# Expert stage on TensorE: the row-column products of the next super between the output products of the preceding one

## What is computed

```python
t = _to_tokens(x)                                 # (32, 3136, 64)
t = t + ffn(_ln_t(t), gate_w, gate_b, w1, b1, w2, b2)

# ffn: every token x goes to the expert with the largest gate probability
idx = argmax(softmax(x @ gate_w + gate_b));  prb = its probability
hmid = relu(buf @ w1 + b1)                        # per expert: 64 -> 256
ybuf = hmid @ w2 + b2                             # per expert: 256 -> 64
y = ybuf[idx, pos] * prb * kept                   # kept: within the capacity
y = nan_to_num(y, nan=0, posinf=1e4, neginf=-1e4)
```

## Time and profile before

| what | value |
|---|---|
| median of 3 runs | 1895.83 us (1888.43 to 1896.14) |
| span of the profiled execution | 2079.0 us |
| expert stage in it, first to last hidden product | 1061.2 to 2036.4 us |
| TensorE busy, whole span | 1654.2 us (80%) |
| VectorE busy | 1482.2 us (71%) |
| ScalarE busy | 1206.3 us (58%) |
| GpSimd busy | 1048.5 us (50%) |
| mean granted TensorE clock, as a share of 2.4 GHz | 0.881 |

### The profile page before, as it was taken

One profiled execution on the slowest core, in us unless ns is written; L12 is line 12 of the kernel. 1 busy time (PEld: TensorE's weight loads), 2 busy tenths in 40 slices (PEclk: granted clock), 3 DMA queues, 4 the chain that ended last, 5 costly groups with the idle time before them and its releaser, 6 DMA issues.

```text
span 2079.0 us, 40865 instructions
## 1 busy us (share of the span) xinstructions
PE 1654.2 (80%) x10341; PEld 880.9 (42%) x10341; DVE 1482.2 (71%) x3641; ACT 1206.3 (58%) x4066; POOL 1048.5 (50%) x1052
## 2 busy tenths in 40 slices
PE   7998888888888878775058888888888888878884
PEld 1344433443333434443034444555555445445453
DVE  3488878878887878888135666787677777777675
ACT  3687877777777877765035554655455454455451
POOL 2116655655676656667524444554444444444442
PEclk7898989988899989886579999999999999999896
DMA  9136766554557554442164555777777677777786
GB/s 240 40 97 145 176 165 157 150 142 117 148 149 135 139 133 108 108 112 78 59 191 142 145 147 144 193 219 244 226 234 230 220 236 225 228 222 228 227 247 221
DMA packets 302207, 351.64 MB, mean 169 GB/s; under 512 B 48452, under 2 KB 252452, under 8 KB 295940
## 3 DMA queue, kind: packets, MB, share of 16 engines
q1 hardware_dynamic: 260644, 264.23, 47.2%
q0 software_dynamic: 41120, 85.81, 13.3%
q10 hardware_dynamic: 320, 0.33, 0.1%
HBM read 179.70 MB, written 180.01 MB: 173 GB/s over the span
## 4 chain that ended last, share of the span: by engine, by line
PE 37%; issue 16%; DVE 14%; another core or an unknown queue 11%; POOL 8%; ACT 6%; DMA 4%; SPq 2%; ACTq 1%; POOLq 0%; DVEq 0%
PE bank L821 9%; PE bank L831 8%; POOL pairs_by_group L490 6%; PE bank L812 3%; PE bank L730 3%; POOL X L484 3%; PE bank L692 2%; PE bank L839 2%; PE bank L789 2%; PE bank L740 2%; DMA X<-weights_by_group 2%; PE bank L763 2%; ACT X L975 2%; DVE Z L1250 1%
## 5 line engine op out<-in xcount | busy, mean ns | idle before, releaser
L521 POOL DMA_INDIRECT results_by_pair<-X,PAIRNO x462 | 461.2, 998 | 542.1 <-ACT X L980 420.6
L490 POOL DMA_INDIRECT pairs_by_group<-ROWS,idx x400 | 435.4, 1088 | 133.2 <-issue 113.9
L821 PE MATMUL bank<-X 64*128 64x256 f32 x1848 | 287.7, 432 | 60.6 <-issue 28.7
L975 ACT ACTIVATE X<-bank,X 128x256 f32<-128x256 f32 x693 | 284.6, 474 | 76.2 <-PE bank L821 58.9
L968 ACT ACTIVATE X<-bank 128x256 f32<-128x256 f32 x231 | 90.5, 392 | 389.9 <-remote 238.1
L484 POOL TENSOR_TENSOR X<-Z,X 128x448 f32 (+1 forms) x112 | 137.0, 1223 | 308.9 <-DVE Z L1266 290.9
L831 PE MATMUL bank<-X 128*64 128x256 f32 x1848 | 276.3, 424 | 6.9 <-ACT X L985 6.9
L812 PE MATMUL bank<-ident,X 128*64 128x128 f32 x1848 | 159.3, 294 | 145.5 <-DMA X<-weights_by_group 69.2
L821 PEld LDWEIGHTS bank<-X 64*128 64x128 f32 x1848 | 180.3, 200 | 114.7 <-issue 103.3
L730 PE MATMUL bank<-S,WB 128*128 128x448 bf16 x1008 | 227.9, 374 | 0.0
L1289 DVE TENSOR_SCALAR X<-bank,X 128x256 f32<-128x256 f32 x231 | 111.1, 481 | 131.8 <-PE bank L821 63.3
(11 more groups left out here) (209 smaller groups left out, 3006.5 us busy)
## 6 DMA issues: line engine op xcount, KB each, us to landing
X<-weights_by_group SPq DMA_DIRECT2D x231, 258.5 KB
X<-pairs_by_group SPq DMA_DIRECT2D x231, 134.0 KB
pairs_by_group<-PAD SPq DMA_DIRECT2D x15, 1742.0 KB
X<-in_x_dram SPq DMA_DIRECT2D x16, 1568.0 KB
block_output<-X SPq DMA_DIRECT2D x112, 224.0 KB, 1.9
ROWS<-block_output SPq DMA_DIRECT2D x16, 1568.0 KB
Z<-results_by_pair SPq DMA_DIRECT2D x16, 1568.0 KB
out_dram<-ROWS SPq DMA_DIRECT2D x16, 1568.0 KB
```

The lines of the kernel that those rows point to most:

```text
L490: pool.indirect_dma_start(rows, bass.IndirectOffsetOnAxis(ap=idx[0:m, p.odd, k:k + 1], axis=0), ROWS[0:m, p.odd, k, :], None).then_inc(s_s ...
L521: pool.indirect_dma_start(done, bass.IndirectOffsetOnAxis(ap=PAIRNO[:, u, j:j + 1], axis=0), RES[:, u, j, :], None,).then_inc(s_back[u], 16)
L821: mm(hidden(q), WR[b, ring, q // 2 * P:(q // 2 + 1) * P], XT[b, ring % 2, :], start=True, stop=True).then_inc(s_h, 1)
L975: last = A(HB[:, ring % 2, q, :], hidden(q), ACT.Relu, bias=WR[:, ring, at:at + 1])
```

## The change

Only TensorE's `super_pass` changes. The hidden products of super k come first in the pass. Behind them the four row-column products of super k+1 and the four output products of super k-1 stand alternately: row-column product 0, output product 0, row-column product 1, and so on. The waits that stood ahead of either group now stand together ahead of the joint one. The row-column product q and the output product q write the same half of the partitions. ScalarE, VectorE, GpSimd and SyncE keep their programs; lines behind the edit have numbers that are 7 higher (ScalarE's 968, 975, 980, 985 become 975, 982, 987, 992).

```diff
             def super_pass(k, ring, t=True, l1=True, l2=True, back=True):
-                if t:
-                    u = (ring + 1) % RING
-                    wait(pe, s_rt[u], (k + 1 - u) * (32 // RING) + 32)
-                    wait_apart(pe, s_xt, k + 1)
-                    for d in range(SUB):
-                        for h in range(2):
-                            last = mm(PT[h * C:h * C + C, d * P:(d + 1) * P], RTH[:, u, d, h, 0:C], ident[:, :],
-                                      start=True, stop=True)
-                    last.then_inc(s_pt, 1)
                 if l1:
                     wait(pe, s_xt, k + 1)
                     wait(pe, s_ha, k)
                     wait(pe, s_hb, k)
                     for q in range(HC):
...
+                if t:
+                    wait(pe, s_rt[u], (k + 1 - u) * (32 // RING) + 32)
+                    wait_apart(pe, s_xt, k + 1)
                 if l2:
                     wait(pe, s_ha, k)
                     wait(pe, s_hb, k)
                     wait(pe, s_ys, k - 1)
-                    for q in range(HC):
...
-                    last.then_inc(s_y, 1)
+                for q in range(HC):
+                    if t:
+                        columns = row_columns(q // 2, q % 2)
+                        if q == HC - 1:
+                            columns.then_inc(s_pt, 1)
+                    if l2:
+                        results = output(q)
+                        if q == HC - 1:
+                            results.then_inc(s_y, 1)
```

More of the change, by code:

```diff
@@ L805, in super_pass, with row_columns, output @@
             def super_pass(k, ring, t=True, l1=True, l2=True, back=True):
-                if t:
-                    u = (ring + 1) % RING
-                    wait(pe, s_rt[u], (k + 1 - u) * (32 // RING) + 32)
-                    wait_apart(pe, s_xt, k + 1)
-                    for d in range(SUB):
-                        for h in range(2):
-                            last = mm(PT[h * C:h * C + C, d * P:(d + 1) * P], RTH[:, u, d, h, 0:C], ident[:, :],
-                                      start=True, stop=True)
-                    last.then_inc(s_pt, 1)
+                u, b = (ring + 1) % RING, (ring - 1) % RING
+                def row_columns(d, h):
+                    return mm(PT[h * C:h * C + C, d * P:(d + 1) * P], RTH[:, u, d, h, 0:C], ident[:, :],
+                              start=True, stop=True)
+                def output(q):
+                    h = q % 2
+                    at = W2_AT + (h * KT + q // 2) * C
+                    return mm(YT[h * C:h * C + C, 0:SUPER], WR[:, b, at:at + C], HB[:, b % 2, q, :],
+                              start=q < 2, stop=q >= HC - 2)
                 if l1:
@@ L819, in super_pass @@
                     for q in range(HC):
-                        b = slice(q % 2 * C, q % 2 * C + C)
-                        mm(hidden(q), WR[b, ring, q // 2 * P:(q // 2 + 1) * P], XT[b, ring % 2, :],
+                        r = slice(q % 2 * C, q % 2 * C + C)
+                        mm(hidden(q), WR[r, ring, q // 2 * P:(q // 2 + 1) * P], XT[r, ring % 2, :],
                            start=True, stop=True).then_inc(s_h, 1)
+                if t:
+                    wait(pe, s_rt[u], (k + 1 - u) * (32 // RING) + 32)
+                    wait_apart(pe, s_xt, k + 1)
                 if l2:
-                    b = (ring - 1) % RING
                     wait(pe, s_ha, k)
@@ L827, in super_pass @@
                     wait(pe, s_ys, k - 1)
-                    for q in range(HC):
[L829 to L832, removed]
-                    last.then_inc(s_y, 1)
+                for q in range(HC):
[7 more added lines that the diff above has]
+                            results.then_inc(s_y, 1)
                 if back:
-                    b = ring % 2
+                    c = ring % 2
                     wait(pe, s_ys, k - 1)
@@ L838, in super_pass @@
                     for d in range(SUB):
-                        last = nc.tensor.transpose(YB[:, d * P:(d + 1) * P], YS[:, b, d * P:(d + 1) * P], ident[:, :])
+                        last = nc.tensor.transpose(YB[:, d * P:(d + 1) * P], YS[:, c, d * P:(d + 1) * P], ident[:, :])
                     last.then_inc(s_yb, 1)
```

## The result

| kernel | median of the runs | lowest to highest |
|---|---|---|
| before | 1895.55 us (4 runs) | 1888.43 to 1896.14 |
| after | 2066.72 us (4 runs) | 2060.85 to 2071.07 |

The ratio of after to before is 1.0878, with a 95% interval from 1.0836 to 1.0919: 171 us slower. The forecast was 2040 us, 1970 to 2140.

The account below looks back on a forecast made before the run. TensorE was taken to bound undisturbed passes; after the change a TensorE-ScalarE circle of 1.07 + 1.22 + 1.56 + 0.09 = 3.94 us a super makes the 792 us stage 935: 1896 + 143, say 2040 us, range 1970 to 2140.

Parts of the forecast that it names:

- What TensorE saves: Joint section empties the array once: 1.44 instead of 1.60 us, pass 2.88 instead of 3.04, 37 us if nothing waited.
- the circle: Expert stage: TensorE's hidden products and ScalarE's copy and relu tiles wait for each other in turn, 3.94 us a super; 75%.
- Step 1: TensorE, start of the hidden products of super k to the start of the joint section: 1.07 us.
- Step 2: Start of TensorE's joint section to the start of ScalarE's columns copy: 0.85 + 0.37 = 1.22 us.
- Step 3: ScalarE, start of the columns copy to the end of the third relu tile: 1.56 us, between 1.48 and 1.65.
- Step 4: End of ScalarE's relu tiles to the TensorE hidden products that wait for them: 0.09 us.
- The strictly written order: Upper bound in the joint section: products starting strictly in written order add 0.21 us a pass; by that rule 2088 us.
- The stage of the kernel before: Expert stage in a run without a profile, inferred as 792 us: the profile's 975 us less 183.
- much of the circle is hidden: Rival, 10%: the expert stage before is longer (900 us), so part of the new wait falls into existing waits; +35, 1930 us.
- The 25 us above the undisturbed sum: Expert stage before: 792 us inferred against 767 us of undisturbed passes; the some 25 us were kept in the forecast stage.
- Halves that no longer overlap: Rival, 8%: the array's halves wait for each other, joint section streams 2.54 us, 5.21 us a super; +437, 2333 us.
- The circle does not bind: Rival, 7%: relu tiles are made before the copy is waited for, so the saved emptying shows; faster, 1859 us.

Follow-up runs that it names:

- the grouped order: Kernel after with all four row-column products ahead of the four output products: 1914.91 us; with ScalarE's relu tiles also ahead of its columns copy: 1887.15 us.
- the order by pairs: Kernel after with joint section as row columns 0, 1, outputs 0, 1, row columns 2, 3, outputs 2, 3, and relu tiles ahead of the columns copy: 1885.69 us.
- The exchange in the order: Kernel after with row-column product 3 put ahead of output product 2 instead of behind it: 1971.66 us, ratio to before 1.0403.
- both repairs: Kernel after with relu tiles ahead of ScalarE's columns copy and TensorE's joint section reordered: 1887.15 us (row columns first) and 1885.69 us (alternating by twos).

## Why the prediction was right, and where it was not

The sign, the mechanism and the range were right; the time was 27 us too low, and that hides two larger errors that went against each other. That it came so near is luck.

- **What TensorE saves.** The joint section was to take 1.44 us. It takes 1.50 in the kernel after (1734.94 to 1736.44), and 1.45 both with the grouped order (1192.85 to 1194.30) and in the order by pairs (1243.86 to 1245.31), which has the same alternation on each half. The fixed part is saved as worked out; the order in which the change writes the products gives 0.05 us of it back. Passes of 2.88 us show where nothing waits, but that is 15 of 230 steps: once the circle is gone, VectorE holds the usual pass at 3.0 us, a limit that the 37 us "if nothing waited" left out.
- **Step 1 of the circle**, 1.07 us: measured 1.07.
- **Step 2 is the term that was mis-sized**: 1.22 us was said, 1.65 measured. The step let the last row-column product be reported when it had run. The exchange in the order gives exactly the 1.22 that was said, since there no unfinished output product stands ahead of it in the written order. The 0.43 us are what it costs that output product 2 stands ahead of it: 231 x 0.43 = 99 us, and the exchange took 95 us off the time.
- **Step 3**, 1.56 us: measured 1.48, the lower of the two rows that it was taken between the earlier trace rows, since the relu tiles now always find their products made. **Step 4**, 0.09: measured 0.09.
- **The strictly written order.** For this bound the prediction added 0.21 us a pass and cited the Trainium skill, page TensorE: Matmul & The Clock Gate, section Part 3, The mechanism: matmuls start and end strictly in program order. By that sentence alone the time was 2088 us. The two parts of it have to be kept apart. The starts are not in order here: all four records of row-column products 0 and 1 start ahead of the first record of output product 0 (1735.21), which is written ahead of product 1. The end of row-column product 3, as its semaphore tells it, is in order: it waits for output product 2. By the rows the time was 2040 us, and the truth lies between the two for a reason that neither had.
- **The stage of the kernel before** was taken at 792 us and is 847 in a profile without the "remote" waits. The rival "much of the circle is hidden" rested on such a longer stage, and that much of it came true: the new pass covers 55 us that were there already.
- **The sum, with these two put right**: 1896 + 231 x 4.29 + 25 - 847 = 2065 us, where 2066.72 was measured. The circle was 81 us too short, the stage 55 us too short, and a longer stage before takes away from the difference, so most of the one cancelled the other. The 25 us above the undisturbed sum were 23.
- **Image groups** were to fall into the pause: right, 4.29 us with and without.
- **The clock** was charged nothing: right. Behind pauses of 0.90 and 1.29 us the hidden products take 1.14 us, and the stage has a granted clock of 0.98.
- **What the profile would show.** ScalarE's copy waits for line 809, by 2.25 us a pass and not 1.4: 0.35 of that is the longer pass, and the rest is that ScalarE's steps in a pass take 2.03 us (1736.59 to 1738.13 + 0.49), where the forecast left 2.54 (3.94 - 1.4). TensorE's wait ahead of the hidden products is some 1 us, 273 us in all, but the page names "issue" for most of it (235.4 us) and not ScalarE. The profiled execution was to take 2222 us if the "remote" waits stayed; they did not, and it took 2066.
- **The rivals.** Halves that no longer overlap: refuted by a joint section of 1.50 us. The circle does not bind: refuted by the passes of 4.29 us. With the relu tiles ahead of the copy, the condition that the rival named, the circle falls to 3.07 us, but not below 2.88. In the sum of *Much of the circle is hidden* the stage scaled like the span is 975 x 1896 / 2079 = 889 us, not 900.

Shown by runs: that the semaphore of row-column product 3 waits for output product 2, written ahead of it on the other half; that the queue on ScalarE makes this costly; and how much each is worth. Shown by the semaphore records: that TensorE's "issue" ahead of the hidden products is the wait for ScalarE's relu tiles. Argued only: that TensorE's semaphores rise in the written order in general. Open: what held up the semaphores in the first profile, why passes with image groups take up to 4.0 us in the second profile of the kernel before, and where the 9 us of the stage come from with both repairs.

## What to carry to other kernels

When a product that another engine waits for is moved in among others, put it ahead of everything that it needn't wait for in the written order, even if it would run at the same time further behind: here its semaphore rose only when the product ahead of it was done, which cost 95 us. Before a producer is moved later in the pass, look at what is queued behind its consumer on that engine, and ask whether the producer's next step waits for that; if so, both engines take turns, and one block moved in the consumer's order can be worth more than a better order of the producer (here 181 us against 152 for the better of the two orders tried alone). And take a second profile of the starting kernel when the first is longer than its runs, before any of the excess is put into one stage.

## What the hardware did that was not expected

- Products on the two column halves started out of the written order (four records of line 809 ahead of the first of line 815 at 1735.21), while the semaphore of one waited for the product written ahead of it. One exchange moved a product's start by 0.04 us and its consumer's start by 0.43 us, and with that the whole kernel by 95 us.
- Alternating two kinds of product on each half costs nothing by itself: the section takes 1.45 us grouped and 1.45 us in the order by pairs, and 1.50 us only in the order of the change.
- A profiled execution can carry waits that no other execution of the same kernel shows: 2079.0 us against 1892.9 us of span, 238 us of them under the name "remote", which were waits for semaphores of TensorE that rose 1.9 to 4.4 us after the row columns' last record had started (0.30 us is usual for `s_pt`).
